# One pass of a graph network kernel: its last sum moves to GpSimd, a bias moves from TensorE to GpSimd and VectorE, and half of a base array stays on chip

## Chip, cores and metric

The kernel runs on one core of one Trainium2 chip. The metric is the device time of one launch in microseconds; the median of several executions counts.

## The reference

`x` has 50,000 nodes of 128 features, and there are 25,000 edges with 64 features and a type. Cut to what matters:

```python
h = relu(layernorm(x))
x = x + rgcn(rgcn(h))                     # two relational layers
h = relu(layernorm(x))
# message network on h, x here is the sum after the first block
msg  = layer_norm(relu(relu(concat(h[src], h[dst], edge) @ eW1 + eb1) @ eW2 + eb2), eg, ebeta)
agg  = segment_sum(msg, dst)
upd  = relu(concat(h, agg) @ nW1 + nb1) @ nW2 + nb2
out  = x + layer_norm(h + upd, ng, nbeta) # (h + upd - mean) * rstd * ng + nbeta
```

All arithmetic is fp32.

## The kernel before, in words

Nodes go in 49 groups of 1024 (`GN`, eight tiles of 128 nodes; the last group overlaps the one before it), edges in 49 groups of 512 (`GE`, four tiles). The kernel is a row of stages, each a block with one program for each engine, and a block ends when all its engines have ended: setup, N0 (node pass), E1 (edge pass), N1, E2, N2, E3 (message pass), N3 (last pass). Within a stage, engines run their programs in order and wait on semaphores that count up.

**Setup.** VectorE splits two bias vectors, `nb2` and `eb2`, in three bf16 parts each (L281 to L294), so that one bf16 matmul with `parts_weight` can add a bias to a whole PSUM bank. GpSimd makes small constants and then issues the first gathers.

**Message pass** (`edge_pass_messages`, groups i, u with g = 4i + u). GpSimd issues indirect DMAs: it gathers `h[dst]` (L1400) and scatters sums into `s3` (L1410). The gathered source rows `gathered` (128 x 25088 fp32, 512 columns for each edge group) were loaded earlier; VectorE uses group g + 2 of them in its step g (`source_rows`), after which these slots aren't read again. Beside this, VectorE makes the base of a node group: `update` (L1448) and `add_nbeta` (L1454) form x + relu(s2) + nbeta in a buffer `base` with two slots, SP loads its inputs (L1365, L1366) and stores the result in DRAM (`store_base`, L1373). SP's program in step g is: load edge rows of g + 3, store base of g - 1, load base inputs of g + 1.

**Last pass** (`node_pass_3`). For each node group g it takes `s3` (`sin`), `h` (`hin`) and `base` from DRAM:

- SP: load(g+4) of sin and hin, which waits for product of g + 1; store(g-1), which waits for out_ready; load_base(g+1).
- TensorE, per group: residual(g, 0), turn(g+1), residual(g, 1), update(g, 0), update(g, 1). `turn` (L880) makes eight transposes of sin. `residual` (L890, L892) puts the bias nb2 and then h into a PSUM bank (`u_bank`, a ring of three groups, which is free after outer_norm of g - 3); `update` (L900) adds hidden @ nW2 to it.
- ScalarE, per group: hidden_rows(g+2, 0), L173 of g (the square root of the variances), hidden_rows(g+2, 1), outer_norm(g). `hidden_rows` (L849) is relu with bias on the transposed rows; `outer_norm` (L191, eight times) normalises from PSUM into `normal`.
- VectorE, per group: halves(g), the statistics of PSUM (L144, eight times), small sums (L151 to L166), scale(g-1, 0), reciprocal (L179) and shift (L185) of g, scale(g-1, 1), finish(g-1, 0), finish(g-1, 1). `scale` (L935) multiplies a half by ng, `finish` (L947) adds the base and makes the result.
- GpSimd does nothing.

The two arguments of hidden_rows, residual, scale and finish are the group and the half (512 columns).

Of the kernel before, what the change touches and what calls it, by code (L numbers as in the profile page):

```python
# [199 lines left out]
def constants(sb):  # L200

    c = {}

    def keep(name, shape, dt=F32):
        c[name] = sb("c_" + name, shape, dt)

    for name in ("ident", "sl1", "nb2", "eb2", "sl2", "eW2", "nW2", "eW1s", "eW1d", "nW1x", "nW1m", "b2", "eg",
                 "ebeta", "ng", "nbeta"):
        keep(name, [P, D])
    keep("eW1e", [DE, D])  # L210
    for name in ("b1", "eb1", "nb1", "eps", "one"):
        keep(name, [P, 1])
    keep("earlier", [P, WINDOW * P])
    for name in ("nb2_parts", "eb2_parts"):
        keep(name, [3 * QUARTER, 4, D], BF16)
    keep("parts_weight", [3 * QUARTER, P], BF16)
    for name in ("src", "dst", "near", "scat"):
        keep(name, [P, TILES_E], I32)
    for name in ("dstf", "dump_less_dst", "dump"):
        keep(name, [P, TILES_E])  # L220
    return c


def setup(nc, sb, sem, c, ps, a, gathers):
# [18 lines left out]
    for name in ("b1", "eb1", "nb1"):  # L243
# [6 lines left out]
    bias_parts = [c["nb2_parts"], c["eb2_parts"]]  # L250
# [4 lines left out]
    with nc.Block() as block:  # L255
# [11 lines left out]
        @block.vector  # L267
        def _(dve):
            nc.vector.memset(eps[:], EPS).then_inc(dve_done, 1)
            nc.vector.memset(one[:], 1.0)  # L270

            dve.wait_ge(loaded, 16 * len(first_loads))
            nc.vector.tensor_copy(dstf[:], dst[:]).then_inc(dve_done, 1)

            dve.wait_ge(dve_done, 2)
            dve.wait_ge(pool_done, 5)
            nc.vector.tensor_tensor(dump_less_dst[:], dump[:], dstf[:], ALU.subtract)
            nc.vector.tensor_scalar(near[:], dst[:], float(NODES - 1), None, ALU.min)
            nc.vector.memset(parts_weight[:], 1.0 / QUARTER)
            done = 2  # L280
            for left, parts in ((c["nb2"], bias_parts[0]), (c["eb2"], bias_parts[1])):  # L281
                for k in range(3):

                    nc.vector.tensor_copy(part[:], left[:]).then_inc(dve_done, 1)
                    dve.wait_ge(dve_done, done + 1)
                    quarter = slice(k * QUARTER, (k + 1) * QUARTER)
                    for j in range(4):
                        ins = nc.vector.tensor_copy(parts[quarter, j, :], part[quarter, :])
                    ins.then_inc(dve_done, 1)
                    nc.vector.tensor_tensor(rest[:], left[:], part[:], ALU.subtract).then_inc(dve_done, 1)  # L290

                    dve.wait_ge(dve_done, done + 3)
                    done += 3
                    left = rest  # L294
# [49 lines left out]
class Gathers:  # L344
# [21 lines left out]

    def group(self, g):
        return self.rows[:, bass.ds(g * GE, GE)]


def node_product(nc, sb, sem, c, ps, a, name, x, s, w, norm, gathers):
# [402 lines left out]
            sweep(pe, step)  # L774


def node_pass_3(nc, sb, sem, c, ps, a):

    S = lambda n: sem(f"N3_{n}")
    U_RING = 3  # L780
# [2 lines left out]
    base = sb("N3_base", [P, 2, NT * D])  # L783
    hidT = sb("N3_hidT", [P, 2, NT * D])
    normal = sb("N3_normal", [P, 2, NT * D])
    scaled = sb("N3_scaled", [P, NT * D])
    res = sb("N3_res", [P, 2, NT * D])
    ln = Stats(sb, sem, "N3", NT)
    loaded = [S(f"loaded{k}") for k in range(UNROLL)]
# [1 line left out]
    stored = [S(f"stored{k}") for k in range(2)]  # L791
    turned, hidT_ready, product = S("turned"), S("hidT_ready"), S("product")
    normed, scaled_ready, out_ready = S("normed"), S("scaled_ready"), S("out_ready")

    def u_bank(g, half):
        return ps[:, 2 + 2 * (g % U_RING) + half, :]
# [7 lines left out]
    with nc.Block() as block:  # L804
        @block.sync
        def _(sp):
            def load(g):
                u = g % UNROLL

                wait(sp, product, 2 * (g - 3))  # L810
                sp.dma_start(sin[:, u, :], rows(a["s3"], at(g))).then_inc(loaded[u], 16)
                sp.dma_start(hin[:, u, :], rows(a["h"], at(g))).then_inc(loaded[u], 16)

            def load_base(g):
                u = g % 2

                wait(sp, out_ready, 2 * (g - 1))
                sp.dma_start(base[:, u, :], rows(a["base"], at(g))).then_inc(based[u], 16)

            def store(g):  # L820
                u = g % 2
                last_store(sp, stored, g)

                sp.wait_ge(out_ready, 2 * g + 2)
                sp.dma_start(rows(a["out"], at(g)), res[:, u, :]).then_inc(stored[u], 16)

            for g in range(UNROLL):
                load(g)
            for g in range(2):
                load_base(g)  # L830
            for g in range(GROUPS_N):
                if g + 4 < GROUPS_N:
                    load(g + 4)
                if g >= 1:
                    store(g - 1)
                    if g + 1 < GROUPS_N:
                        load_base(g + 1)
            store(GROUPS_N - 1)
            all_stored(sp, stored)
# [33 lines left out]
        def _(pe):  # L873
# [11 lines left out]
            def residual(g, half):  # L885
                u = g % UNROLL
                if half == 0:

                    wait(pe, normed, 2 * (g - 2))
                nc.tensor.matmul(u_bank(g, half), c["parts_weight"][:], c["nb2_parts"][:].rearrange("p k d -> p (k d)"),  # L890
                                 start=True, stop=False, skip_group_check=True)
                nc.tensor.matmul(u_bank(g, half), c["ident"][:], hin[:, u, half * 512:(half + 1) * 512],  # L892
                                 start=False, stop=False, skip_group_check=True)

            def update(g, half):

# [17 lines left out]
        def _(dve):  # L914
# [14 lines left out]
            def scale(g, half):  # L929
# [1 line left out]

                dve.wait_ge(normed, 2 * g + half + 1)
                if half == 0:
                    wait(dve, out_ready, 2 * g)
                nc.vector.tensor_tensor(tiles_of(scaled[:, cols]), tiles_of(normal[:, g % 2, cols]),  # L935
                                        each_tile(c["ng"], NT // 2), ALU.mult).then_inc(scaled_ready, 1)

            def finish(g, half):
                u = g % 2
                cols = slice(half * 512, (half + 1) * 512)  # L940
                if half == 0:

                    dve.wait_ge(based[u], 16 * (g // 2 + 1))
                    wait(dve, stored[u], 16 * (g // 2))

                dve.wait_ge(scaled_ready, 2 * g + half + 1)
                nc.vector.tensor_tensor(res[:, u, cols], scaled[:, cols], base[:, u, cols],  # L947
                                        ALU.add).then_inc(out_ready, 1)

            for g in range(GROUPS_N):  # L950
                halves(g)
                statistics(g)
# [2 lines left out]
                scales(g)  # L955
                if g:
                    scale(g - 1, 1)
                    finish(g - 1, 0)
                    finish(g - 1, 1)
            for half in range(2):  # L960
                scale(GROUPS_N - 1, half)
            for half in range(2):
                finish(GROUPS_N - 1, half)


def edge_pass_relational(nc, sb, sem, c, ps, a, name, x, s, w, norm, gathers):
# [347 lines left out]
def edge_pass_messages(nc, sb, sem, c, ps, a, sources):  # L1314
# [24 lines left out]
    base_stored = [S(f"base_stored{k}") for k in range(2)]  # L1339
    base_step = S("base_step")  # L1340
    turned, turned_out, hidden_product = S("turned"), S("turned_out"), S("hidden_product")
    hidden_ready, msg_product, msg_ready = S("hidden_ready"), S("msg_product"), S("msg_ready")
    normal_step, same_ready = S("normal_step"), S("same_ready")
    pair_product, summedT_ready, out_product, summed_ready = (
        S("pair_product"), S("summedT_ready"), S("out_product"), S("summed_ready"))

    with nc.Block() as block:
        @block.sync
        def _(sp):
# [11 lines left out]

            def load_base(i, u):

                wait(sp, base_stored[u % 2], 16 * (2 * i + u // 2))
                sp.dma_start(base[:, u % 2, :], rows(a["s2"], node_base(i, u))).then_inc(base_loaded[u % 2], 16)  # L1365
                sp.dma_start(base_x[:, u % 2, :], rows(a["x"], node_base(i, u))).then_inc(base_loaded[u % 2], 16)  # L1366

            def store_base(i, u):
                g = UNROLL * i + u
                last_store(sp, base_stored, g)  # L1370

                sp.wait_ge(base_step, 2 * g + 2)
                sp.dma_start(rows(a["base"], node_base(i, u)), base[:, u % 2, :]).then_inc(base_stored[u % 2], 16)  # L1373

            def step(i, u):
                if first(i, u):
# [10 lines left out]

            sweep(sp, step)
            store_base(GROUPS_N // UNROLL, 0)
            all_stored(sp, base_stored)  # L1390

        @block.gpsimd
        def _(pool):
# [31 lines left out]
        def _(dve):  # L1425
# [31 lines left out]
            def equalities(i, u):  # L1457
# [200 lines left out]
def graph_layers(nc, ctx, a):  # L1658
# [17 lines left out]
    with ExitStack() as edges:  # L1676
# [13 lines left out]
    stage(node_pass_3)  # L1690


# [41 lines left out]
```

## Time and profile before

| | us |
|---|---|
| median of 3 runs (2732.85 to 2799.01) | 2733.24 |
| profiled execution, its own time | 2735.0 |
| its span, first to last instruction | 2733.3 |
| busy: TensorE, VectorE, ScalarE, GpSimd | 2139.7, 2024.7, 1544.4, 1788.3 |
| moved by DMA (MB, GB/s over the span) | 563.74, 206 |

The mean granted TensorE clock is 0.929 of 2.4 GHz. The kernel has stages with different limits, so the shares over the whole span say little about one stage; the last pass runs from the first load at 2461.88 to the end, 271 us. In the profile DVE is VectorE, ACT ScalarE, PE TensorE (PEld its weight loads), POOL GpSimd, SPq the queue from which SP issues DMAs. L12 is line 12 of the kernel; lines 144 to 196 are helpers for the layer norms.

### The profile page before, as it was taken

How to read it: one execution, taken by the hardware profiler on the slowest of the kernel's cores; microseconds unless marked ns; L12 is line 12 of the kernel's file. 1: busy time of each engine (PE TensorE's matmuls, PEld its weight loads, DVE VectorE, ACT ScalarE, POOL GpSimd, SP SyncE). 2: the span in 40 equal slices, each digit the busy share in tenths (PEclk: the TensorE clock that was granted, in tenths of full speed). 3: DMA queues.
4: the chain of work that ended last, by engine and by line, in shares of the span. 5: the costliest groups of instructions: out<-in, count | busy, mean ns of one | idle time of the engine just before them, and what ended most of it. 6: DMA issues, size and time to landing. Idle time of an engine off the chain costs nothing. (4 is left out here: it accounts for less than half of the span.)

```text
span 2733.3 us, 54746 instructions
## 1 busy us (share of the span) xinstructions
PE 2139.7 (78%) x16219; PEld 1874.0 (69%) x16219; DVE 2024.7 (74%) x6853; ACT 1544.4 (57%) x3284; POOL 1788.3 (65%) x1381
## 2 busy tenths in 40 slices
PE   3777999999588898888891656577777777648997
PEld 3667999999577798888891655544455544436775
DVE  6887888888333587666662888688777777747999
ACT  4997666666333354444442888645444444426887
POOL 7771777776577188888876777568888888860000
PEclk9999999999899999999995898889888899879999
DMA  6994455555299634444545999877777777739998
GB/s 210 318 323 161 96 103 107 109 109 107 31 340 358 215 73 76 77 85 79 82 56 141 406 417 417 341 230 218 196 189 206 197 200 196 201 72 352 408 409 339
DMA packets 296009, 563.74 MB, mean 206 GB/s; under 512 B 88628, under 2 KB 145377, under 8 KB 295905
## 3 DMA queue, kind: packets, MB, share of 16 engines
q1 hardware_dynamic: 186144, 484.03, 50.9%
q0 software_dynamic: 109760, 78.51, 18.2%
q8 instruction: 43, 0.70, 0.1%
q14 instruction: 62, 0.50, 0.1%
HBM read 368.35 MB, written 205.52 MB: 210 GB/s over the span
## 5 line engine op out<-in xcount | busy, mean ns | idle before, releaser
L1049 POOL DMA_INDIRECT s<-E_summed,c_scat x392 | 637.4, 1626 | 250.9 <-issue 101.5
L1278 PE MATMUL ps<-c_w,E_masked 128*128 128x128 f32 x6272 | 720.4, 276 | 3.9 <-DVE E_masked L1081 3.8
L1278 PEld LDWEIGHTS ps<-c_w,E_masked 128*128 128x128 f32 x6272 | 711.8, 193 | 4.7 <-DVE E_masked L1081 4.7
L1081 DVE SCALAR_TENSOR_TENSOR E_masked<-E_type_row,E_hT 128x512 f32<-128x512 int32 x784 | 483.2, 687 | 78.0 <-ACT E_hT L1198 64.8
L358 POOL DMA_INDIRECT gathered<-s,c_src x392 | 419.0, 1069 | 166.7 <-issue 116.1
L1410 POOL DMA_INDIRECT s<-E_summed,c_scat x196 | 337.4, 1722 | 85.5 <-issue 58.2
L1400 POOL DMA_INDIRECT E_ends<-h,c_near x196 | 202.6, 1034 | 75.8 <-issue 56.1
L358 POOL DMA_INDIRECT gathered<-in_x,c_src x196 | 189.6, 967 | 88.0 <-issue 58.8
L564 PE MATMUL ps<-c_sl,N_hT 128*128 128x128 f32 x1568 | 195.3, 278 | 19.4 <-DVE N_out L399 17.8
L1293 PE MATMUL ps<-E_msg,E_same 128*128 128x128 bf16 (+1 forms) x2450 | 207.3, 241 | 1.2 <-DVE E_msg L1131 1.2
L564 PEld LDWEIGHTS ps<-c_sl,N_hT 128*128 128x128 f32 x1568 | 183.4, 192 | 28.3 <-ACT N_hT L513 21.3
L1293 PEld LDWEIGHTS ps<-E_msg,E_same 128*128 128x128 bf16 (+1 forms) x2450 | 199.5, 136 | 1.9 <-DVE E_msg L1131 1.3
L550 PE MATMUL ps<-c_ident,N_xin 128*128 128x128 f32 x784 | 107.3, 282 | 118.6 <-ACT N_xin L191 80.5
L1208 ACT ACTIVATE E_same<-E_dst_row,c_dstf 128x128 f32<-128x128 int32 (+7 forms) x392 | 188.2, 557 | 2.3 <-DMA E_dst_row<-in_dst_line 2.3
L748 PE MATMUL ps<-c_ident,N_h 128*128 128x128 f32 x392 | 66.6, 325 | 151.9 <-ACT N_h L191 151.9
L1229 ACT COPY E_summed<-ps 128x512 f32<-128x512 f32 x98 | 57.7, 588 | 217.3 <-DMA s<-E_summed,c_scat 214.0
L550 PEld LDWEIGHTS ps<-c_ident,N_xin 128*128 128x128 f32 x784 | 89.3, 144 | 127.9 <-issue 91.5
L399 DVE TENSOR_TENSOR N_out<-ps,c_b 128x512 f32<-128x512 f32 x98 | 63.2, 686 | 145.9 <-DMA s<-N_out 84.9
L191 ACT ACTIVATE N_h<-N_sin,N_ln_shift,N_ln_rstd 128x128 f32<-128x128 f32 x392 | 156.1, 481 | 17.1 <-DVE N_ln_shift L185 16.9
L748 PEld LDWEIGHTS ps<-c_ident,N_h 128*128 128x128 f32 x392 | 52.4, 165 | 161.9 <-issue 92.7
L1591 PEld LDWEIGHTS ps<-c_ident,E_ends 128*128 128x128 f32 x392 | 56.3, 173 | 140.8 <-issue 130.0
L1591 PE MATMUL ps<-c_ident,E_ends 128*128 128x128 f32 x392 | 71.3, 341 | 102.1 <-DMA E_ends<-h,c_near 85.9
(133 smaller groups left out, 4461.7 us busy)
## 6 DMA issues: line engine op xcount, KB each, us to landing
s<-N_out SPq DMA_DIRECT2D x147, 512.0 KB, 4.7
N_xin<-in_x SPq DMA_DIRECT2D x98, 512.0 KB, 10.1
N_sin<-s SPq DMA_DIRECT2D x98, 512.0 KB, 6.9
E_dst_row<-in_dst_line SPq DMA_DIRECT2D x147, 256.0 KB, 4.7
E_type_row<-in_type SPq DMA_DIRECT2D x98, 256.0 KB, 4.0
N_xin<-s SPq DMA_DIRECT2D x49, 512.0 KB, 6.4
h<-N_h SPq DMA_DIRECT2D x49, 512.0 KB, 7.8
E_base<-s SPq DMA_DIRECT2D x49, 512.0 KB
```

The source lines that it names most:

```text
L191: return nc.scalar.activation(out, in_, func, bias=self.tile(self.shift, slot, k), scale=self.tile(self.rstd, slot, k))
L358: pool.indirect_dma_start(self.rows[:, self.issued * D:(self.issued + 1) * D], None, table, bass.IndirectOffsetOnAxis(ap=self.index[:, sel ...
L550: ins = nc.tensor.transpose(ps[:, 2 * (u % 2) + k // 4, (k % 4) * P:(k % 4 + 1) * P], xin[:, u, k * D:(k + 1) * D], c["ident"][:])
L564: ins = nc.tensor.matmul(ps[:, 4 + 2 * (u % 2) + h, k * D:(k + 1) * D], hT[:, u % 2, at:at + P], w[:], start=True, stop=True)
L1049: pool.indirect_dma_start(s, bass.IndirectOffsetOnAxis(ap=c["scat"][:, k:k + 1], axis=0), summed[:, g % 2, t * D:(t + 1) * D], None, bound ...
L1081: nc.vector.scalar_tensor_tensor(out=masked[:, u % 2, r, :], in0=type_row[:, u, :], scalar=float(r), in1=hT[:, u % 2, :], op0=ALU.is_equal ...
L1208: ins = nc.scalar.activation(same_block(same[:, u % 2, :], t, 0, t + 1), dst_row[:, u, 0:(t + 1) * P], ACT.Square, bias=c["dstf"][:, bass. ...
L1278: ins = nc.tensor.matmul(ps[:, 2 + u % 2, t * D:(t + 1) * D], masked[:, u % 2, r, t * P:(t + 1) * P], w[:, r, :], start=(r == 0 and t == 0 ...
L1293: ins = nc.tensor.matmul(ps[:, 4 + u % 2, t * D:(t + 1) * D], same_block(same[:, u % 2, :], s, t, t + 1), msg[:, u % 2, p, s * D:(s + 1) * D],
L1400: pool.indirect_dma_start(ends[:, u, GE + t * D:GE + (t + 1) * D], None, a["h"], bass.IndirectOffsetOnAxis(ap=c["near"][:, k:k + 1], axis= ...
L1410: pool.indirect_dma_start(a["s3"], bass.IndirectOffsetOnAxis(ap=c["scat"][:, k:k + 1], axis=0), summed[:, g % UNROLL, t * D:(t + 1) * D], ...
L1591: nc.tensor.transpose(ps[:, t // GT, (t % GT) * P:(t % GT + 1) * P], ends[:, u, t * D:(t + 1) * D], c["ident"][:])
```

## The change

In the last pass:

- The bias nb2 is added to h in place in `hin`: the first half of the columns by GpSimd, the second by VectorE, both two groups ahead. TensorE's two bias matmuls (L890) go, and residual waits for `first_biased` or `second_biased`. The bf16 parts of nb2 go from the setup.
- GpSimd makes the last sum as one instruction on 128x1024; VectorE's `finish` goes. `scaled` gets two slots.
- The base of each odd group isn't stored by the message pass and not loaded by the last pass. The message pass writes it into `gathered`, over rows of two edge groups that were used already, and the last pass reads it there. `gathered` therefore lives on into the last pass.

```diff
-    for name in ("nb2_parts", "eb2_parts"):
+    for name in ("eb2_parts",):
...
+def kept_base(row_buffer, k):
+    return row_buffer[:, bass.ds(k * NT * D, NT * D)]
...
-def node_pass_3(nc, sb, sem, c, ps, a):
+def node_pass_3(nc, sb, sem, c, ps, a, kept):
...
-    scaled = sb("N3_scaled", [P, NT * D])
+    scaled = sb("N3_scaled", [P, 2, NT * D])
...
+    def base_of(g):
+        return kept_base(kept, g // 2) if g % 2 else base[:, g // 2 % 2, :]
+    def add_bias(engine, g, half):
+        cols = slice(half * 512, (half + 1) * 512)
+        rows_here = tiles_of(hin[:, g % UNROLL, cols])
+        return engine.tensor_tensor(rows_here, rows_here, each_tile(c["nb2"], NT // 2), ALU.add)
...
             def load_base(g):
-                u = g % 2
-                wait(sp, out_ready, 2 * (g - 1))
+                u = g // 2 % 2
+                wait(sp, out_ready, g - 3)
...
-                sp.wait_ge(out_ready, 2 * g + 2)
+                sp.wait_ge(out_ready, g + 1)
...
-                    if g + 1 < GROUPS_N:
+                    if g % 2 and 3 <= g + 1 < GROUPS_N:
                         load_base(g + 1)
...
                     wait(pe, normed, 2 * (g - 2))
-                nc.tensor.matmul(u_bank(g, half), c["parts_weight"][:], c["nb2_parts"][:]...)
+                    pe.wait_ge(first_biased, g + 1)
+                else:
+                    pe.wait_ge(second_biased, g + 1)
+                nc.tensor.matmul(u_bank(g, half), c["ident"][:], hin[:, u, half * 512:(half + 1) * 512],
                                  start=True, stop=False, skip_group_check=True)
-                nc.tensor.matmul(u_bank(g, half), c["ident"][:], hin[:, u, half * 512:(half + 1) * 512],
-                                 start=False, stop=False, skip_group_check=True)
...
-            def finish(g, half):
...
+            def bias(g):
+                dve.wait_ge(loaded[g % UNROLL], 32 * (g // UNROLL + 1))
+                add_bias(nc.vector, g, 1).then_inc(second_biased, 1)
+            for g in range(2):
+                bias(g)
             for g in range(GROUPS_N):
                 halves(g)
                 statistics(g)
...
                 scales(g)
                 if g:
                     scale(g - 1, 1)
-                    finish(g - 1, 0)
-                    finish(g - 1, 1)
+                if g + 2 < GROUPS_N:
+                    bias(g + 2)
...
+        @block.gpsimd
+        def _(pool):
+            def bias(g):
+                pool.wait_ge(loaded[g % UNROLL], 32 * (g // UNROLL + 1))
+                add_bias(nc.gpsimd, g, 0).then_inc(first_biased, 1)
+            def finish(g):
+                u = g % 2
+                if g % 2 == 0:
+                    pool.wait_ge(based[g // 2 % 2], 16 * (g // 4 + 1))
+                wait(pool, stored[u], 16 * (g // 2))
+                pool.wait_ge(scaled_ready, 2 * g + 2)
+                nc.gpsimd.tensor_tensor(res[:, u, :], scaled[:, u, :], base_of(g), ALU.add).then_inc(out_ready, 1)
+            for g in range(2):
+                bias(g)
+            for g in range(GROUPS_N):
+                if g + 2 < GROUPS_N:
+                    bias(g + 2)
+                finish(g)
...
 # edge_pass_messages
+    def base_of(i, u):
+        return kept_base(sources.rows, 2 * i + u // 2) if u % 2 else base[:, 0, :]
...
             def load_base(i, u):
-                wait(sp, base_stored[u % 2], 16 * (2 * i + u // 2))
+                if u % 2:
+                    wait(sp, base_step, 2 * (UNROLL * i + u - 1))
+                else:
+                    wait(sp, base_stored, 16 * (2 * i + u // 2))
...
             def store_base(i, u):
+                if u % 2:
+                    return
...
-                nc.vector.scalar_tensor_tensor(out=base[:, u % 2, :], in0=base[:, u % 2, :], scalar=0.0,
+                nc.vector.scalar_tensor_tensor(out=base_of(i, u), in0=base[:, u % 2, :], scalar=0.0,
...
-                nc.vector.tensor_tensor(tiles_of(base[:, u % 2, :]), tiles_of(base[:, u % 2, :]),
+                nc.vector.tensor_tensor(tiles_of(base_of(i, u)), tiles_of(base_of(i, u)),
                                         each_tile(c["nbeta"], NT), ALU.add).then_inc(base_step, 1)
```

## Rows read from the trace of the kernel before

**Rows 1.** The page's busy tenths in 40 slices of 68.3 us, VectorE and GpSimd

```profile
DVE  6887888888333587666662888688777777747999
...
POOL 7771777776577188888876777568888888860000
```

**Rows 2.** Last pass, 50 us: busy PE, PEld, DVE, ACT, POOL; granted clock, DMA share, GB/s

```profile
2500.00:2550.00 50.00, 47.52 (x288) 34.82 (x287) 48.63 (x199) 42.38 (x107) 0.00 (x0) 1.00 1.02 407
```

**Rows 3.** Timeline (start, us, ...; bracketed: idle before), last pass's first and last statistics

```profile
2474.53 1.68 DVE L144 BATCH_NORM_STATS2 N_ln_st<-ps 128x6 f32<-128x128 f32 x8 [44.24 <-PE ps L900]
...
2721.93 1.67 DVE L144 BATCH_NORM_STATS2 N_ln_st<-ps 128x6 f32<-128x128 f32 x8
```

**Rows 4.** Timeline, one steady group of the last pass

```profile
2603.40 0.38 PE L890 MATMUL ps<-c_nb_parts,c_parts_weight 96*128 96x512 bf16 x1
...
2603.62 1.02 PE L892 MATMUL ps<-N_hin,c_ident 128*128 128x512 f32 x2
...
2605.78 0.30 ACT L173 ACTIVATE N_ln_sd<-N_ln_var,c_eps 128x8 f32<-128x8 f32 x1 [0.76 <-DVE N_ln_var L166]
...
2606.26 0.20 DVE L179 RECIPROCAL N_ln_rstd<-N_ln_sd 128x8 f32<-128x8 f32 x1
...
2606.58 0.69 DVE L935 TENSOR_TENSOR N_scaled<-N_normal,c_ng 128x512 f32<-128x512 f32 x1
...
2607.18 1.29 DVE L947 TENSOR_TENSOR N_res<-N_scaled,N_base 128x512 f32<-128x512 f32 x2
...
2608.38 1.68 DVE L144 BATCH_NORM_STATS2 N_ln_st<-ps 128x6 f32<-128x128 f32 x8
```

**Rows 5.** Timeline, the last pass's first groups, where engines wait for each other

```profile
2476.50 1.02 PE L892 MATMUL ps<-N_hin,c_ident 128*128 128x512 f32 x2
...
2477.09 0.30 ACT L173 ACTIVATE N_ln_sd<-N_ln_var,c_eps 128x8 f32<-128x8 f32 x1 [0.30 <-DVE N_ln_var L166]
...
2477.36 1.95 PE L900 MATMUL ps<-c_nW,N_hidT 128*128 128x128 f32 x16
...
2477.42 0.20 DVE L179 RECIPROCAL N_ln_rstd<-N_ln_sd 128x8 f32<-128x8 f32 x1 [0.37 <-ACT N_ln_sd L173]
...
2480.23 1.03 PE L880 MATMUL ps<-c_ident,N_sin 128*128 128x128 f32 x8
...
2480.92 0.69 ACT L849 ACTIVATE N_hidT<-ps,c_nb 128x512 f32<-128x512 f32 x1 [0.16 <-PE ps L880]
...
2481.75 0.19 PEld L900 LDWEIGHTS ps<-c_nW,N_hidT 128*128 128x128 f32 x1 [0.24 <-ACT N_hidT L849]
```

**Rows 6.** Timeline, GpSimd's only arithmetic, in the setup

```profile
0.32 0.10 POOL L1724 MEMSET const-float32-0.0<- 128x1 f32 x1 [0.32 <-issue]
...
1.73 0.28 POOL L302 TENSOR_SCALAR_AFFINE_SELECT c_ident<-c_ident 128x128 f32<-128x128 f32 x1 [0.24 <-POOL c_earlier L299]
1.97 0.60 POOL L305 TENSOR_SCALAR_AFFINE_SELECT c_earlier<-c_earlier 128x512 f32<-128x512 f32 x1
2.55 0.52 POOL L308 IOTA c_dump<- 128x196 f32 x1
```

**Rows 7.** Timeline of node pass 2; then lines L358, L1448 (xcount: ns min/median/max)

```profile
1603.09 1.23 DVE L647 SCALAR_TENSOR_TENSOR N_sin<-N_sin,N_xin 128x1024 f32<-128x1024 f32 x1 [0.75 <-DMA N_xin<-in_x]
...
1603.53 1.60 POOL L358 DMA_INDIRECT gathered<-s,c_src  x1 [0.30 <-issue]
...
L358 POOL DMA_INDIRECT gathered<-s,c_src x392: 940/947/1992, 754.0 to 1753.8; - x196
...
L1448 DVE SCALAR_TENSOR_TENSOR E_base<-E_base,E_base_x x49: 1210/1218/1227, 1793.0 to 2422.2; 128x1024 f32<-128x1024 f32 x49
```

**Rows 8.** The same view, 30 us of node pass 2

```profile
1680.00:1710.00 30.00, 17.09 (x127) 15.86 (x125) 25.56 (x100) 24.42 (x60) 23.57 (x21) 0.90 1.03 417
```

**Rows 9.** Timeline, VectorE's first work after the setup

```profile
30.01 1.65 DVE L144 BATCH_NORM_STATS2 N_ln_st<-N_xin 128x6 f32<-128x128 f32 x8 [13.84 <-DMA N_xin<-in_x]
```

**Rows 10.** The same view, 100 us of the message pass

```profile
2200.00:2300.00 100.00, 70.60 (x320) 45.97 (x318) 79.79 (x282) 44.85 (x99) 81.71 (x61) 0.95 0.76 199
```

More of the change, by code:

```diff
@@ L249, in setup @@
         c[k] for k in ("src", "dst", "near", "dstf", "dump_less_dst", "dump"))
-    bias_parts = [c["nb2_parts"], c["eb2_parts"]]
     loaded, pool_done, dve_done = sem("loaded"), sem("pool_done"), sem("dve_done")
@@ L280, in _ @@
             done = 2
-            for left, parts in ((c["nb2"], bias_parts[0]), (c["eb2"], bias_parts[1])):
+            for left, parts in ((c["eb2"], c["eb2_parts"]),):
                 for k in range(3):
@@ L793, in node_pass_3 @@
     normed, scaled_ready, out_ready = S("normed"), S("scaled_ready"), S("out_ready")
+    first_biased, second_biased = S("first_biased"), S("second_biased")
+    def base_of(g):
[4 more added lines that the diff above has]
+        return engine.tensor_tensor(rows_here, rows_here, each_tile(c["nb2"], NT // 2), ALU.add)
     def u_bank(g, half):
@@ L829, in _ @@
             for g in range(2):
-                load_base(g)
+                load_base(2 * g)
             for g in range(GROUPS_N):
@@ L889, in residual @@
                     wait(pe, normed, 2 * (g - 2))
-                nc.tensor.matmul(u_bank(g, half), c["parts_weight"][:], c["nb2_parts"][:].rearrange("p k d -> p (k d)"),
+                    pe.wait_ge(first_biased, g + 1)
+                else:
+                    pe.wait_ge(second_biased, g + 1)
+                nc.tensor.matmul(u_bank(g, half), c["ident"][:], hin[:, u, half * 512:(half + 1) * 512],
                                  start=True, stop=False, skip_group_check=True)
-                nc.tensor.matmul(u_bank(g, half), c["ident"][:], hin[:, u, half * 512:(half + 1) * 512],
-                                 start=False, stop=False, skip_group_check=True)
             def update(g, half):
@@ L933, in scale @@
                 if half == 0:
-                    wait(dve, out_ready, 2 * g)
-                nc.vector.tensor_tensor(tiles_of(scaled[:, cols]), tiles_of(normal[:, g % 2, cols]),
+                    wait(dve, out_ready, g - 1)
+                nc.vector.tensor_tensor(tiles_of(scaled[:, g % 2, cols]), tiles_of(normal[:, g % 2, cols]),
                                         each_tile(c["ng"], NT // 2), ALU.mult).then_inc(scaled_ready, 1)
-            def finish(g, half):
[L939 to L948, printed above, removed]
+            def bias(g):
[3 more added lines that the diff above has]
+                bias(g)
             for g in range(GROUPS_N):
@@ L957, in _ @@
                     scale(g - 1, 1)
-                    finish(g - 1, 0)
-                    finish(g - 1, 1)
+                if g + 2 < GROUPS_N:
+                    bias(g + 2)
             for half in range(2):
                 scale(GROUPS_N - 1, half)
-            for half in range(2):
-                finish(GROUPS_N - 1, half)
+        @block.gpsimd
[16 more added lines that the diff above has]
+                finish(g)
 def edge_pass_relational(nc, sb, sem, c, ps, a, name, x, s, w, norm, gathers):
@@ L1338, in edge_pass_messages @@
     base_loaded = [S(f"base_loaded{k}") for k in range(2)]
-    base_stored = [S(f"base_stored{k}") for k in range(2)]
+    base_stored = S("base_stored")
     base_step = S("base_step")
@@ L1369, in store_base @@
                 g = UNROLL * i + u
-                last_store(sp, base_stored, g)
+                if u % 2:
+                    return
+                if isinstance(g, int) and g == GROUPS_N - 1:
+                    sp.wait_ge(base_stored, 16 * (g // 2))
                 sp.wait_ge(base_step, 2 * g + 2)
-                sp.dma_start(rows(a["base"], node_base(i, u)), base[:, u % 2, :]).then_inc(base_stored[u % 2], 16)
+                sp.dma_start(rows(a["base"], node_base(i, u)), base[:, u % 2, :]).then_inc(base_stored, 16)
             def step(i, u):
@@ L1389, in _ @@
             store_base(GROUPS_N // UNROLL, 0)
-            all_stored(sp, base_stored)
+            sp.wait_ge(base_stored, 16 * (GROUPS_N // 2 + 1))
         @block.gpsimd
@@ L1689, in graph_layers @@
         stage(edge_pass_messages, sources)
-    stage(node_pass_3)
+        stage(node_pass_3, gathered)
 _WEIGHTS = {
```

## The prediction

> **What bounds the kernel now.** I read the page's busy tenths first [rows 1]. The change touches the last pass (the last 4 of 40 slices), one edit in the pass before it, and one item of the setup. In the last pass GpSimd shows 0 and VectorE up to 9. Next I read a stretch of 50 us in it [rows 2]: VectorE is busy 48.63 us, TensorE 47.52, ScalarE 42.38, GpSimd 0, and the DMA share is 1.02 at 407 GB/s. Four resources are nearly full and one is empty.
>
> Then the timeline gives the period. VectorE's first statistics of the pass start at 2474.53, its last at 2721.93 [rows 3]: 48 periods of 5.154 us. In a steady group [rows 4] VectorE goes from the reciprocal (2606.26) to the second half of the scaling (2606.58), the last sum L947 (2607.18) and the next statistics (2608.38) with no idle time in brackets, while ScalarE waited 0.76 us for it before L173. So VectorE sets the end.
>
> **The change by its busy times.** This is the sum if one counts work only.
> - VectorE loses L947 twice (2607.18 to 2608.38, 1.20 us) and gains one 128x512 sum at the start spacing of such instructions (L935 to L947, 0.60): 5.15 - 0.60 = 4.55 a group.
> - TensorE loses two L890, each 0.22 before L892 [rows 4]. Its 47.52 of 50 us are 4.90 a group: 4.90 - 0.44 = 4.46.
> - ScalarE keeps its work: 5.15 - 0.76 = 4.39.
> - DMA moves 3.5 transfers of 0.524 MB instead of 4: 1.835 MB at 407 GB/s [rows 2] is 4.51.
> - GpSimd gets a 128x1024 and a 128x512 sum, priced below. Even dear they leave it room.
>
> By this count the period would be about 4.6 us and the kernel 0.56 x 48 = 27 us shorter. I do not forecast that, because the new waits close a ring.
>
> **The ring.** I follow who waits for whom, in program order on each engine:
> 1. VectorE: reciprocal(g) waits for ScalarE's L173 of g. Behind it stand shift(g) and then scale(g-1, 1).
> 2. GpSimd: finish(g-1) waits for scale(g-1, 1). Behind it in the same queue stands bias(g+2), although its data landed long ago.
> 3. TensorE: residual(g+2, 0) now waits for first_biased of g+2. Behind it stands turn(g+3), which needs no bias.
> 4. ScalarE: hidden_rows(g+3, 0) waits for turn(g+3), and L173 of g+1 stands behind it. That is step 1 of the next group.
>
> One turn of this ring is one period. Before, TensorE's residual waited only for ScalarE's outer_norm of three groups earlier, so no such ring was closed. Its terms:
> - VectorE: L173 to the reciprocal that waits for it, 2477.09 to 2477.42 [rows 5], 0.33; reciprocal to scaling 0.32 and the scaling 0.69 [rows 4]. Together 1.34.
> - GpSimd's start: 0.24 after a semaphore in the setup (L302, [rows 6]). But VectorE starts its own bias(g+2) 0.60 after the scaling began, before that has ended; it reads two tensors in SBUF and takes 0.69. What GpSimd does beside such a sum is in [rows 7]: the median DMA issue takes 0.947, the one that starts at 1603.53, within L647 (1603.09 to 1604.32), takes 1.60. It is longer by 0.65, nearly what was left of L647 (0.79). So I let finish(g-1) start when VectorE's bias ends, 0.60 after the scaling's end.
> - finish and bias: the trace shows no two-input arithmetic on GpSimd. The nearest rows are in [rows 6]. Affine_select, one input, takes 0.28 for 128 columns and 0.60 for 512: 0.83 ns a column and 0.18 fixed. At that rate finish is 1.03 and bias 0.60, together 1.63: the lower bound. Iota takes 0.52 for 196 columns, 2.65 ns each with its fixed part; then finish is 2.72 and bias 1.36, together 4.08: the upper bound. I choose near the upper end, because a sum has one stream more to serve than affine_select: the iota's rate less 0.10, a memset of one column, which is 2.14 ns a column. Finish 0.10 + 2.19 and bias 0.10 + 1.10 are 3.49.
> - TensorE and ScalarE [rows 5]: from the releasing engine's end to the weight load 0.14 (L849 ends 2481.61, L900 loads at 2481.75), load to matmul 0.22 (as L890 to L892, [rows 4]), residual to the next group of matmuls 0.86 (L892 2476.50, L900 2477.36), turn to hidden_rows 0.69 (L880 2480.23, L849 2480.92), hidden_rows itself 0.69. Together 2.60.
>
> Sum: 1.34 + 0.60 + 3.49 + 2.60 = 8.03 us. Everything counted above is shorter. Without GpSimd's two sums and without the delay by VectorE's bias the ring is 8.03 - 3.49 - 0.36 = 4.18; with the lower bound of 1.63 it is 5.81, still above 5.15. So no price inside the bounds makes the last pass shorter.
>
> TensorE would be busy about 4.5 of 8 us. Where it is busy 17.09 of 30 us, the granted clock is 0.90 [rows 8], a mixture of the 2.4 and 1.2 GHz levels, against 1.00 in [rows 2]. At 0.90 the 1.6 us of TensorE in the ring grow by 0.18. I take 8.2 us a period.
>
> Apart from the sum, a page gives a price: the Trainium skill, GPSIMD Engine Reference, section Performance versus the Vector engine, has 4497 ns for a GpSimd tensor_tensor add of 2048 fp32 columns. By it finish and bias would be an estimated 3.4 us and the period 8.1. The trace has no row for this.
>
> The ring acts where a finish lies before and a bias remains, g = 1 to 46: 46 x (8.2 - 5.15) = 140 us. The two other periods, at 4.55, give back 1. The last finish costs 2.29 instead of the 1.29 of L947 (x2) [rows 4], and takes that 1 again. The first bias (1.2) lies beside the first turn.
>
> **The other edits.** The setup loses three rounds of casts, copies and a subtraction on VectorE. VectorE then idles 13.84 us anyway until its first load at 30.01 [rows 9], because the pass starts only when GpSimd has issued its gathers; without that cover the three of six rounds would be worth at most half of the 16.2 us (30.01 - 13.84) before. I take 0. In the message pass 24 of 49 stores of 0.524 MB go. GpSimd sets that pass: 81.71 us busy in 100, in 61 instructions [rows 10] with 0.30 of issue before each (as in [rows 7]), 18.3, is all of it. The stores are hidden behind it; if all 12.6 MB were in the way, they would be worth 31 us at 407 GB/s. I take 0. VectorE's two base sums keep their shapes. SP loses a store and its wait for odd groups, and the loads behind it come no later. In the last pass SP's store(g-1) waits for GpSimd, with load(g+5) behind it, which has more than two long periods until turn(g+5). With half of the base loads gone and long periods, DMA has slack.
>
> **Sum.** The profiled span is 2733.3, its own time 2735.0, the median of the runs 2733.24. On the median: 2733 + 140 = 2873 us.
>
> **Rivals.**
> - *GpSimd's sums are cheap.* At 1.63 together the period is 5.8 to 6.2, by whether finish waits for VectorE's bias: 2733 + 46 x 0.85 = 2772, within 2%. For it: affine_select's rate. Against: that has one input. Up to 6.34 us the result stays within 2%. Chance 0.10.
> - *VectorE is held too.* If a GpSimd sum keeps VectorE's two-input instructions waiting, the small ones of the statistics and scale(g, 0) (from the statistics at 2608.38 to the next reciprocal, one period after 2606.26, are 3.03 us [rows 4], of which the statistics take 1.68 and these 1.3) squeeze in between finish and bias, and bias waits for them: up to 1.3 more, 9.5 a period, 2733 + 46 x 4.35 = 2933. For it: the mirror of L647's case. Against: L1448 stayed at 1210 to 1227 ns in 49 cases beside GpSimd's issues [rows 7]; but those read no tensor. Chance 0.15. The Trainium skill has such a rule (SBUF — State Buffer, section Who interferes with whom): a VectorE instruction with two SBUF inputs and a GpSimd instruction that reads SBUF exclude each other for the whole instruction. By this rule it would be 2933. The trace agrees in one direction only.
> - *The other side: the ring stays open and the count of work holds.* If GpSimd is so quick that its bias is there before TensorE asks, the period is 4.6 and the kernel 2733 - 27 = 2706. It decides below 5.15 - 4.18 = 0.97 us for both sums. For it: VectorE's and DMA's loads do fall. Against: affine_select on 512 columns alone takes 0.60, and both sums have 1536. Chance 0.04.
>
> The forecast (6.9 to 8.9 us a period) has 0.71.
>
> **How the numbers follow.** The time is the likeliest case's, 2873. Its own span: GpSimd's sums from 2.9 (two inputs at 0.83 ns a column each, 0.18 fixed) to 4.08, with or without the 0.36 and the clock: 6.9 to 8.9, so 2813 to 2906. The range reaches into the dear case and toward the cheap one: 2800 to 2930. This kernel's measurement tells about 2% (55 us) from no change. Slower than 2788 needs a period over 6.34: the forecast, the held case and a little of the cheap one, 0.87. Within 2%: most of the cheap case and the open one, 0.11. Faster by over 2% needs a period under 4.0, below ScalarE's 4.39: 0.02.
>
> **What would show it.** In the new profile the last pass takes about 410 us instead of 271; VectorE's statistics start every 8 us; GpSimd's 128x1024 sum is near 2.3 and the 128x512 near 1.2, back to back; TensorE's first-half L892 waits for GpSimd's bias, ScalarE's L849 for TensorE's L880, VectorE's reciprocal for ScalarE's L173; the DMA share is near 0.6. Setup and message pass are unchanged. The forecast is wrong if GpSimd's bias(g+2) ends before TensorE reaches residual(g+2, 0), or if VectorE still has no wait in a group.

## The result

The changed kernel takes 2884.41 us at the median of 4 runs (2878.75 to 2935.37). The kernel before, run beside it, takes 2738.51 at the median of 4 (2732.85 to 2799.01). The slowest run of each was over 50 us longer than its others, for the kernel before too, so the ratio leaves these two out. It is 1.0532, 95% interval 1.0499 to 1.0565: slower by 5.3%. 2873 was forecast, with 2800 to 2930 as its range.

The profiled span is 2882.3 us, 149 more than before. The last pass's first load is issued at 2473.83, 12 us later than before, so 137 us are in the last pass (408.5 instead of 271.4). The 12 us arose ahead of the message pass, whose first `E_edge` load comes at 1782.2 instead of 1770.8 us; there the change touches only the setup. The message pass itself is the same, 601.1 us from its first to its last `E_edge` load against 600.8. Single executions differ that much: three runs of the kernel before took 2732.85, 2733.24 and 2743.79, and the kernels of experiments 1 to 4, whose code ahead of the last pass is the changed kernel's, issue its first load of `h` at 2465.0, 2491.9, 2462.2 and 2464.4, against 2474.2 here and 2462.3 before.

In 100 us of the last pass all five engines now have room (columns: busy PE, PEld, DVE, ACT, POOL, granted clock, DMA share, GB/s; [rows 2] had 48.63 of 50 for VectorE and a DMA share of 1.02):

```profile
2500.00:2600.00 100.00, 68.48 (x363) 50.67 (x361) 64.63 (x234) 54.51 (x141) 47.78 (x25) 0.90 0.65 229
```

Nothing is full and everything waits. The waits between 2520 and 2850 us name the ring (engine and line, what it waited for, total us, times, longest):

```profile
POOL N_res L987 <- DVE N_scaled L949: 173.3, 41, 5.5
ACT N_hidT L862 <- PE ps L893: 157.2, 41, 5.1
...
PE ps L906 <- POOL N_hin L806: 105.1, 41, 3.1
DVE N_ln_rstd L179 <- ACT N_ln_sd L173: 68.7, 41, 3.1
```

Each of these four waits occurs 41 times in the 330 us: once a group. GpSimd waits for VectorE's scaling, TensorE for GpSimd's bias, ScalarE for TensorE's transposes, VectorE for ScalarE's L173, and the next scaling stands behind that wait. One turn in the timeline (start, us; lines 862, 893, 906, 914 are what 849, 880, 892, 900 were, 949 is the scaling, 806 the bias on either engine, 987 GpSimd's last sum):

```profile
2701.87 0.29 ACT L173 ACTIVATE N_ln_sd<-N_ln_var,c_eps 128x8 f32<-128x8 f32 x1
...
2702.19 0.20 DVE L179 RECIPROCAL N_ln_rstd<-N_ln_sd 128x8 f32<-128x8 f32 x1 [2.78 <-ACT N_ln_sd L173]
...
2702.51 0.68 DVE L949 TENSOR_TENSOR N_scaled<-N_normal,c_ng 128x512 f32<-128x512 f32 x1
...
2703.12 0.69 DVE L806 TENSOR_TENSOR N_hin<-N_hin,c_nb 128x512 f32<-128x512 f32 x1
2703.37 2.64 POOL L987 TENSOR_TENSOR N_res<-N_scaled,N_base 128x1024 f32<-128x1024 f32 x1 [5.23 <-DVE N_scaled L949]
...
2705.97 1.26 POOL L806 TENSOR_TENSOR N_hin<-N_hin,c_nb 128x512 f32<-128x512 f32 x1
...
2707.37 1.10 PE L906 MATMUL ps<-N_hin,c_ident 128*128 128x512 f32 x2 [1.66 <-POOL N_hin L806]
...
2708.31 1.04 PE L893 MATMUL ps<-c_ident,N_sin 128*128 128x128 f32 x8
...
2709.01 0.69 ACT L862 ACTIVATE N_hidT<-ps,c_nb 128x512 f32<-128x512 f32 x1 [3.44 <-PE ps L893]
...
2709.59 0.29 ACT L173 ACTIVATE N_ln_sd<-N_ln_var,c_eps 128x8 f32<-128x8 f32 x1
```

From L173 to L173 are 7.72 us: 1.32 to the scaling's end, 0.18 to GpSimd's start, 2.60 and 1.26 for its two sums, 0.14 to TensorE's matmul, 0.94 to the transposes, 0.70 to L862, 0.58 to L173. The mean period is 7.98 (statistics from 2486.02 to 2869.08 in 48 periods). The next turn of the same timeline shows where the rest is:

```profile
2715.09 2.04 PE L906 MATMUL ps<-N_hin,c_ident 128*128 128x512 f32 x2 [3.10 <-POOL N_hin L806]
...
2716.92 1.91 PE L893 MATMUL ps<-c_ident,N_sin 128*128 128x128 f32 x8
...
2718.37 0.69 ACT L862 ACTIVATE N_hidT<-ps,c_nb 128x512 f32<-128x512 f32 x1 [5.12 <-PE ps L893]
...
2718.96 0.29 ACT L173 ACTIVATE N_ln_sd<-N_ln_var,c_eps 128x8 f32<-128x8 f32 x1
```

The same two steps of TensorE take 1.83 and 1.45 instead of 0.94 and 0.70. Its granted clock is 0.50 from 2715.0 to 2718.3, the lower level of 1.2 GHz, after an idle time of 3.10 us; from 2707.3 to 2709.2 it is 1.00. The turn is 9.37 us. Of the 48 periods from L173 to L173 (2488.58 to 2871.64), 45 are turns of the ring: 26 take 7.71 to 7.74 us, 9 take 7.84 to 8.36, and 10 take 8.70 to 9.37. In each of the 19 longer turns TensorE's two steps take 1.76 to 3.28 instead of 1.64, and that is all that they are longer by, to 0.02 us (0.18 in the first). So the clock falls in part or all of 19 turns of 45, and their mean is 8.12. The three periods at the ends of the pass are shorter (4.38, 6.05, 7.45), which gives the mean of 7.98.

### The profile page after: what moved, and what is told of

The parts are those of the page before. It is cut to its first block and busy times, and to the rows that moved or that the text cites. A ratio compares the mean times of both kernels' runs of the same rounds, so it can differ in the third digit from the quotient of the medians.

```text
span 2882.3 us, 54556 instructions
## 1 busy us (share of the span) xinstructions
PE 2164.8 (75%) x16121; PEld 1890.4 (66%) x16121; DVE 2034.5 (71%) x6786; ACT 1538.9 (53%) x3284; POOL 1974.5 (69%) x1479
## 5 line engine op out<-in xcount | busy, mean ns | idle before, releaser
L906 PE MATMUL ps<-N_hin,c_ident 128*128 128x512 f32 x196 | 129.1, 747 | 120.4 <-POOL N_hin L806 120.4
L862 ACT ACTIVATE N_hidT<-ps,c_nb 128x512 f32<-128x512 f32 x98 | 67.0, 684 | 210.9 <-PE ps L893 210.9
```

## The experiments

Periods below are from the first to the last group's statistics (L144) in the last pass, divided by 48. Before: 5.154. Changed: 7.98.

**1. The ring made twice as long** (`a_bias_ahead3`). The same work in another order.

```diff
-            for g in range(2):
+            for g in range(3):
                 bias(g)
             for g in range(GROUPS_N):
-                if g + 2 < GROUPS_N:
-                    bias(g + 2)
+                if g + 3 < GROUPS_N:
+                    bias(g + 3)
                 finish(g)
```

> Edit: GpSimd issues bias(g+3) instead of bias(g+2) before finish(g). The work is the same, only the ring is longer: scale(g-1,1), finish(g-1), bias(g+3), residual(g+3,0), turn(g+4), hidden_rows(g+4,0), L173(g+2), which is two periods. Ring theory: the 8.1 us of one turn are spread over two periods, 4.1 each, so VectorE (4.55 plus what GpSimd's reads hold it up, some 0.6 a group by the mean 0.78 of L151) sets the end: period 4.9 to 5.3, kernel 2720 to 2745 against 2733 of before. Rival (GpSimd's two sums or the shared access to SBUF cost the time by themselves, wherever they stand in the order): the period stays near 8, kernel near 2880.

Measured: 2782.65 us, ratio 1.0171 (1.0138 to 1.0204), period 5.99. Issuing the bias one group earlier gives back about 100 of the 146 us. So the order closes the ring, and the rival that GpSimd's work costs all of this wherever it stands falls. But the period is 0.7 over the top of what was expected. VectorE is busy 97.7 of 100 us, and its groups by line say with what (busy us, mean ns | idle before; 2500 to 2750 us):

```profile
L153 DVE TENSOR_TENSOR N_ln_small<-N_ln_st 128x8 f32<-128x8 f32 x41 | 50.8, 1239 | 0.0
...
L151 DVE TENSOR_TENSOR N_ln_small<-N_ln_st 128x8 f32<-128x8 f32 x41 | 25.3, 617 | 1.4
```

An addition of 8 columns takes 1.24 us on average. The timeline of this kernel shows why:

```profile
2620.62 2.64 POOL L987 TENSOR_TENSOR N_res<-N_scaled,N_base 128x1024 f32<-128x1024 f32 x1 [2.19 <-DVE N_scaled L949]
...
2622.68 0.62 DVE L151 TENSOR_TENSOR N_ln_small<-N_ln_st 128x8 f32<-128x8 f32 x1
...
2623.23 1.28 POOL L806 TENSOR_TENSOR N_hin<-N_hin,c_nb 128x512 f32<-128x512 f32 x1
...
2623.30 1.24 DVE L153 TENSOR_TENSOR N_ln_small<-N_ln_st 128x8 f32<-128x8 f32 x1
```

L151 starts within GpSimd's sum and ends with it (2623.30 against 2623.26); then GpSimd's bias begins and L153 lasts until that ends (2624.54 against 2624.51). Over their usual 0.17, the two are 0.45 and 1.07 too long: 1.52 a group. The count 4.55 plus 1.52 is 6.07, and in this stretch L151 starts every 6.08 us (2616.60, 2622.68, 2628.76).

**2. TensorE's order changed** (`b_turn_first`).

```diff
-                residual(g, 0)
                 if g + 1 < GROUPS_N:
                     turn(g + 1)
+                residual(g, 0)
                 residual(g, 1)
```

> Edit: TensorE issues turn(g+1) before residual(g,0) instead of behind it, so turn no longer waits for GpSimd's bias. GpSimd's order is as in the changed kernel. Ring theory: the one-period ring is cut at TensorE; left is the ring over two periods: GpSimd 0.2 + 2.6 + 1.3, wake of TensorE 0.36, both residuals and update 3.7, statistics to the second half of the scaling 4.0, together 12.2, 6.1 a period: kernel near 2733 + 46 x 0.95 = 2777. Rival (the wait of update for the bias is what counts, not the turn behind it): the period stays near 8, near 2880.

Measured: 2844.06 us in one run, period 6.73. So the turn behind residual carried 1.25 us a period. The kernel's time is a poor witness here, because its last pass begins 18 to 35 us later than in the others (first load of `h` at 2491.9 against 2456.8 to 2474.2). The 6.1 expected was short by 0.6. Two things were left out of the sum: VectorE is held here too (L151 and L153 take 385 and 685 ns on average from 2550 to 2800 us instead of 170), and the granted clock is 0.88 in 2550 to 2650 us. How the 0.6 divides between them wasn't separated.

**3. GpSimd's bias made twice** (`c_double_bias`).

```diff
-                    pe.wait_ge(first_biased, g + 1)
+                    pe.wait_ge(first_biased, 2 * (g + 1))
...
+                wait(pool, first_biased, 2 * g)
+                nc.gpsimd.tensor_tensor(tiles_of(spare[:]), tiles_of(hin[:, g % UNROLL, 0:512]),
+                                        each_tile(c["nb2"], NT // 2), ALU.add).then_inc(first_biased, 1)
                 add_bias(nc.gpsimd, g, 0).then_inc(first_biased, 1)
```

> Edit: GpSimd makes each bias sum twice, the first time into a spare tile, then in place; the output is unchanged. Ring theory: each period grows by one such sum, 1.26 us, and perhaps 0.1 between them: 46 x 1.3 = +60 on the changed kernel's 2884, so near 2944. Rival (GpSimd has room, being busy 48% in the last pass, and something else sets the 8 us): near 2884.

Measured: 2957.57 us in one run, 73 over the changed kernel, period 9.71. An engine that is busy about half of the time is on the path with all that it does: the added sum of 1.26 us moved the period by 1.73. A turn at TensorE's higher level, from L173 at 2631.90 to the one at 2640.84, is 8.94, so 1.22 more than the changed kernel's 7.72, which is the added sum (from its start at 2636.00 to the next one's at 2637.22). The rest is turns at the lower level: 8 turns take 8.93 to 8.96 and 27 take 10.31 to 10.33, and the clock is 0.84 in 2550 to 2650 us. TensorE waits for GpSimd's bias up to 4.3 us in a turn here, up to 3.1 in the changed kernel (2520 to 2850 us).

**4. The whole bias on VectorE** (`d_vector_bias`): GpSimd makes only the last sum, VectorE adds nb2 to 128x1024.

```diff
-                    pe.wait_ge(first_biased, g + 1)
-                else:
                     pe.wait_ge(second_biased, g + 1)
...
-                add_bias(nc.vector, g, 1).then_inc(second_biased, 1)
+                rows_here = tiles_of(hin[:, g % UNROLL, :])
+                nc.vector.tensor_tensor(rows_here, rows_here, each_tile(c["nb2"], NT), ALU.add).then_inc(second_biased, 1)
...
-                if g + 2 < GROUPS_N:
-                    bias(g + 2)
                 finish(g)
```

> Edit: VectorE makes the whole bias (128x1024, 1.2 us at its start spacing) and GpSimd only the last sum. Ring theory: no ring leads through GpSimd. VectorE's own work is 5.15 a group as before, and the ring through its bias is 1.25 + 1.2 + 2.6 = 5.05. If GpSimd's sum doesn't hold VectorE: 2733. If it does, GpSimd starts behind VectorE's bias and reads for 2.34 us, so the small ones of the statistics (1.68 after the bias) wait 0.7: 5.85 a period, 2765. Rival (moving the last sum to GpSimd costs by itself): over 2800.

Measured: 2756.25 us, ratio 1.0073 (1.0052 to 1.0095), period 5.48. The ring through GpSimd is gone and with it 7.98 - 5.48 = 2.50 of the period. What is left over 5.15 is VectorE held by GpSimd's sum: L151 takes 0.62 instead of 0.17 and ends with it.

```profile
2624.37 1.22 DVE L954 TENSOR_TENSOR N_hin<-N_hin,c_nb 128x1024 f32<-128x1024 f32 x1
2624.60 3.20 POOL L981 TENSOR_TENSOR N_res<-N_scaled,gathered 128x1024 f32<-128x1024 f32 x1 [2.34 <-DVE N_scaled L947]
...
2627.22 0.61 DVE L151 TENSOR_TENSOR N_ln_small<-N_ln_st 128x8 f32<-128x8 f32 x1
```

That is 0.45 a group, less than the 0.7 worked out; VectorE's bias in one instruction is 0.06 shorter from start to start than the two sums that it replaces (1.14 against 1.20), and such a group takes 5.53. The same rows show the other direction: GpSimd's sum, which overlaps VectorE's bias by 0.99 us, takes 3.20 instead of the 2.34 that it takes alone in the changed kernel.

**5. GpSimd's reads or its writes?** The kernel before, with work on GpSimd that nobody waits for: once a sum of 128x1024 a group (`g_before_plus_reads`), once a memset of 128x2560 (`h_before_plus_writes`).

```diff
+                pool.wait_ge(product, 2 * g + 2)
+                pool.wait_ge(spared, g + 1)
+                nc.gpsimd.tensor_tensor(spare[:], fixed[:], fixed[:], ALU.add).then_inc(spared, 1)
```

In the second kernel the last line is instead:

```diff
+                nc.gpsimd.memset(spare[:], 0.0).then_inc(spared, 1)
```

> Edit: the kernel before with a GpSimd sum of 128x1024 a group in the last pass, from a constant tile into a spare tile; nobody waits for it. If a GpSimd read and a VectorE instruction with two SBUF inputs exclude each other, VectorE, which has no slack here, is held by up to 2.34 us less what falls beside the 1.68 us of statistics from PSUM: 0.6 to 2.3 a group, kernel 2760 to 2845. If they don't exclude each other: 2733.

> Edit: as the one with reads, but GpSimd only fills a spare tile of 128x2560 (a memset, about 2.2 us by 0.83 ns a column), so it writes and reads nothing. If only GpSimd's reads hold VectorE's second input: 2733, period 5.15. If any GpSimd instruction on SBUF does: as with reads, 2760 to 2845.

Measured: with reads 2803.98 us in one run, period 6.69; with writes 2737.85 in one run, period 5.154, as before. GpSimd's sum takes 1.89 to 2.39 us a group, its memset 2.23. With reads, one group of the timeline:

```profile
2625.85 2.98 DVE L949 TENSOR_TENSOR N_res<-N_scaled,N_base 128x512 f32<-128x512 f32 x2
2625.91 2.38 POOL L973 TENSOR_TENSOR N_spare<-N_fixed 128x1024 f32<-128x1024 f32 x1 [6.95 <-PE ps L902]
```

The two last sums take 2.98 together, against 1.29 in [rows 4]: 1.69 more. The first began ahead of GpSimd's sum, the second can end only after GpSimd is done at 2628.29. This happens in 21 of the 49 groups. In 20 others GpSimd's sum of 1.89 begins just ahead of L159, and that grows instead:

```profile
2630.72 1.89 POOL L973 TENSOR_TENSOR N_spare<-N_fixed 128x1024 f32<-128x1024 f32 x1 [2.43 <-PE ps L902]
2630.83 1.80 DVE L159 TENSOR_SCALAR N_ln_mean<-N_ln_small 128x8 f32<-128x8 f32 x1
```

The two cases come to (21 x 1.69 + 20 x 1.65) / 48 = 1.43 us a period, and the period grew by 1.54. With the memset of 2.23 us beside them:

```profile
2619.92 2.23 POOL L973 MEMSET N_spare<- 128x2560 f32 x1 [2.75 <-PE ps L902]
2620.32 1.29 DVE L949 TENSOR_TENSOR N_res<-N_scaled,N_base 128x512 f32<-128x512 f32 x2
```

So GpSimd's sum, which reads and writes, holds VectorE, and its memset, which only writes, doesn't. Most of VectorE's instructions that grew in these timelines (L151, L153, the last sums) have two inputs in SBUF. But L159 has one, and is recorded with 1.80 to 1.90 instead of 0.17 in those 20 groups, so two inputs aren't the whole condition. Statistics from PSUM beside the same GpSimd sum keep their 1.68.

**6. The bias back on TensorE** (`e_finish_only`): the changed kernel with the bias as TensorE's L890 made it before. The last sum stays on GpSimd and half of the base on chip.

```diff
-                    pe.wait_ge(first_biased, g + 1)
-                else:
-                    pe.wait_ge(second_biased, g + 1)
+                nc.tensor.matmul(u_bank(g, half), c["parts_weight"][:], c["nb2_parts"][:].rearrange("p k d -> p (k d)"),
+                                 start=True, stop=False, skip_group_check=True)
...
-                if g + 2 < GROUPS_N:
-                    bias(g + 2)
...
-                if g + 2 < GROUPS_N:
-                    bias(g + 2)
                 finish(g)
```

> Edit: the changed kernel with the bias back on TensorE (L890's bf16 matmuls), so GpSimd makes only the last sum and half of the base stays on chip. Nothing leads from GpSimd back to TensorE. VectorE's work is 5.15 - 1.20 = 3.95 a group; GpSimd's sum (2.34 us, started 0.2 after the scaling) outlasts the 1.68 us of statistics by 0.9 and holds VectorE's small instructions for that: 4.85. TensorE's count is 4.82. Theory (ring through the bias was the loss, held VectorE a smaller one): period 4.85 to 4.95, kernel 10 to 14 us under before. Rival (the move of the last sum itself loses): above before, as the kernel with the whole bias on VectorE (period 5.48) still does.

Measured: 2740.39 us, ratio 1.0002 (0.9986 to 1.0017), period 5.05. VectorE is relieved (79.31 us busy from 2500 to 2600) and the time stays. Its waits between 2550 and 2700 us name what came instead:

```profile
DVE N_ln_st L144 <- PE ps L913: 27.9, 29, 3.0
PEld ps L893 <- DMA N_hin<-h: 16.6, 14, 3.3
```

TensorE waits for loads and VectorE for TensorE. SP issues load(g+5) behind store(g-1), and that store now waits for GpSimd. (The load's own wait ends earlier than the description of the kernel says: load(g+4) waits for the product of g, not of g+1.)

**7. Only the base kept on chip** (`f_base_only`): before, with the odd groups' bases in the used row slots and nothing moved between engines.

```diff
+    def base_of(g):
+        return kept_base(kept, g // 2) if g % 2 else base[:, g // 2 % 2, :]
...
+    def base_of(i, u):
+        return kept_base(sources.rows, 2 * i + u // 2) if u % 2 else base[:, 0, :]
```

> Edit: the kernel before with only the kept base: odd groups' bases stay on chip, VectorE makes the last sum, TensorE the bias. VectorE keeps its 5.15 us a group, the message pass is GpSimd's. Theory: no change, within 3 us of before; the DMA share of the last pass falls from 1.02 to 0.89. Rival (a nearly full DMA sets the pass too, or the stores of the message pass are on the path): 10 to 30 us faster.

Measured: 2740.27 us, ratio 1.0030 (1.0006 to 1.0054), period 5.16. Taking 24 of 49 stores and loads away gained nothing. The DMA share is 0.98 instead of 1.02, not the 0.89 expected from the bytes, though 356 GB/s are 0.87 of 407.

**8. The load no longer behind the newest store** (`i_late_store`), on top of experiment 6: three result slots, and SP stores one group later.

```diff
-    res = sb("N3_res", [P, 2, NT * D])
+    res = sb("N3_res", [P, 3, NT * D])
...
-                if g >= 1:
-                    store(g - 1)
+                if g >= 2:
+                    store(g - 2)
```

> Edit: as the kernel with only the last sum on GpSimd, but SP issues store(g-2) instead of store(g-1) behind load(g+4), with three result slots, so the load no longer stands behind a wait for GpSimd's newest sum. In that kernel TensorE waited for loads before L893, up to 3.3 us at a time, and the period was 5.05 instead of the 4.85 counted. Theory (load behind the store's wait): the load waits go, period 4.85 to 4.95, 10 us under before, ratio 0.996. Rival (the DMA itself, share 0.98 there, sets the loads): unchanged, ratio 1.000.

Measured: 2722.19 us, ratio 0.9950 (0.9937 to 0.9964), period 4.80. This beats both kernels, and the only step from experiment 6 is where SP's store stands, with the slot that it needs. TensorE is now full, and no wait for a load is among the waits between 2550 and 2700 us:

```profile
2500.00:2600.00 100.00, 100.00 (x626) 77.44 (x625) 81.34 (x376) 92.71 (x229) 48.28 (x22) 1.00 1.01 382
```

The kernel before with this later store alone wasn't run. VectorE has no wait in it from 2480 to 2720 us, so it should gain little, but that is argued, not shown.

## Why the prediction was right

**What bounds, and that the count of work misleads.** Right. By work the last pass should have come to 4.6 us a group. It went to 7.98, with every engine under 70% busy from 2500 to 2600 us.

**The ring.** Right in each link: the four waits, 41 times in 41 groups. That these orders close it is shown by changing only the order: on GpSimd it gives back about 100 us (experiment 1), on TensorE 1.25 us a period (2). That GpSimd's sums are on the path with their whole duration is shown by experiment 3.

**The terms.** Forecast 8.03 at full clock, measured 7.72:
- VectorE's part: 1.34, measured 1.32.
- GpSimd's last sum with its start: 0.60 + 2.29 = 2.89, measured 0.18 + 2.60 = 2.78. The form was a little different. GpSimd isn't shown as waiting for VectorE's bias; it starts at 0.18 and takes 2.63 to 2.73 beside it, in the first 46 groups, but 2.34 or 2.35 in the last three, where no such sum runs. So the overlap with VectorE's bias costs 0.30, near the 0.36 forecast. The row that the forecast took for this didn't stand for all: another of GpSimd's issues isn't longer beside such an instruction (the one at 1849.58 in the message pass before takes 0.95, L1448 runs from 1849.75 to 1850.97).
- GpSimd's bias: 1.20, measured 1.26. The iota's rate, chosen near the upper bound, came out right: 2.34 for 1024 and 1.26 for 512 columns are 2.11 ns a column, against 2.14. As a reading of the rows that was luck, since an iota adds nothing and has no input. Affine_select's 0.83 would have given 1.63 for both instead of 3.6. By the Trainium skill (GPSIMD Engine Reference, section Performance versus the Vector engine) both were an estimated 3.4; the trace agrees within 0.2.
- TensorE and ScalarE: 2.60, measured 2.36. A weight load of 0.22 was counted (from L890's start to L892's, which are two matmuls), but none stands in the path: the matmul comes 0.14 after GpSimd's end. L862 to L173 is 0.58, not 0.69.
- The clock: 0.18 was taken, 0.40 measured (8.12 - 7.72). The mean granted clock of 0.90 that the forecast took is that of 2500 to 2600 us; over 2470 to 2870 it is 0.87. Its cost fell unevenly, on 19 turns by up to 1.65.

In all 46 turns of 8.2 were forecast and 45 of 8.12 measured. That is closer than the terms: at full clock the ring was 0.31 too long, for the clock 0.22 too short, and the two cancel by chance. The last pass grew by 137 instead of 140 us. The profiled span is 9 over the 2873 because in that execution the last pass began 12 later. One end of the stated span is off in its sum: 4.18 and 2.9 are 7.1 a period (2822 us), not 6.9 (2813). The measurement is far from it.

**The other edits at nothing.** Right: experiment 7 has the base alone at 1.003, and the message pass kept its length. The setup's edit wasn't run alone. Nothing was gained where a full DMA share seemed to promise it.

**The rivals.** *Cheap sums* fell by the duration of the sums. *VectorE is held too* was right as a mechanism and wrong in its consequence here. In the changed kernel L151, 0.17 long where nothing holds it, takes 0.78 on average (2480 to 2890 us):

```profile
L151 DVE TENSOR_TENSOR N_ln_small<-N_ln_st 128x8 f32<-128x8 f32 x49 | 38.3, 782 | 1.7
```

But VectorE then waits for L173 anyway (77.1 us in these 410), and GpSimd goes from its last sum to its bias without a gap, so the hold falls into waiting time. Its price shows as soon as the ring is open: 1.52 a group in experiment 1. There the mistake was mine: I expected 0.6, the mean hold of a kernel in which VectorE mostly waits. By the Trainium skill's rule (SBUF — State Buffer, section Who interferes with whom) both directions were to be expected, and experiments 1, 4 and 5 agree: a sum of GpSimd holds a VectorE instruction with two SBUF inputs to its end (L153 1.24 instead of 0.17 us), such an instruction makes a GpSimd sum longer (3.20 instead of 2.34), and a memset holds nothing. That L159, with one input, grew too isn't in the rule as told here. *The ring stays open* fell.

**What the changed kernel would have needed.** Not less work: another order. With the bias left on TensorE, whose 0.44 us a group it wanted to save, and SP's load freed from the newest store, the same move of the last sum and the same kept base are worth 0.5% together (experiment 8).

## What to carry to other kernels

Before work moves to an idle engine, write down for each new wait what stands behind the waiting instruction in its queue, and follow it until it either ends or comes back to the start. If it comes back within one period, the period can't be shorter than the sum of all durations on that ring, however idle each engine looks; issuing one item a group earlier can open it. GpSimd's sums here take twice VectorE's time (1.26 against a start spacing of 0.60 for 512 columns, 2.34 against 1.20 for 1024), and while they run they hold VectorE's instructions with two inputs in SBUF, even those of 8 columns, and in experiment 5 one with a single input (L159).

## What the runs showed of the hardware beyond the forecast

A held VectorE instruction isn't shown as idle time: it is shown as busy and long (L153 with 8 columns at 1239 ns in experiment 1), so "busy" of 97.7 in 100 us held 1.52 of each 6.07 us in which VectorE was only held. A group's mean duration against that of the kernel before shows it at once. And a mean granted clock of 0.90 was not a slightly slower engine but a part of the turns at the lower level: TensorE's two steps took 3.28 instead of 1.64 us in the turn wholly at it, and something between in 18 others. The turn at the lower level shown above began after TensorE had idled 3.10 us, but other turns of the same pass with the same idle time before L906 (the one at 2555.51, say) stayed at the higher one; what picks them isn't settled here.
